# Scatters of routed rows, one at a time and spaced by TensorE's progress, in a metaformer layer with a mixture of experts

## The chip, the cores and the metric

One NeuronCore of a Trainium2 chip. The metric is the device time of one execution, in microseconds.

## The reference

```python
x = x + conv_ref(ln_c(x), ...)      # x is 2 x 256 x 96 x 96, float32
t = to_tokens(x)                    # 18432 tokens of 256 channels
t = t + ffn_ref(ln_t(t), ...)
# conv_ref: four branches, dilation 1, 4, 8, 12: a 3x3 convolution to 9 channels, softmax over
# the 9, then each pixel's 3x3 dilated patch weighted by them; [x, 4 branches] through a
# 1280 -> 256 projection, group norm (32 groups), relu
# ffn_ref: router to 8 experts, top 2 with weights normed to sum 1;
# expert: gelu(t @ w1[e] + b1[e]) @ w2[e] + b2[e]
```

## The kernel before

The program is written by hand, engine by engine, with semaphores between the engines. For each image m (0 and 1) there are two stages. The first norms the channels, makes the taps of the 36 filter channels, their softmax and the first fifth of the projection. The second, the convolution stage, has 64 steps (`STEPS`): each step weights the patches of one branch for one block of pixels on TensorE and projects the result. A step is made of units, four to six, 288 units (`UNITS`) per image; a unit ends with TensorE raising `out_ready`, after which ScalarE evicts it into `cat_hi` (L1423) and VectorE into `cat_lo` (L1941). Patches stand in a ring of 3 and are loaded by SyncE and, for part of them, by GpSimd (L2183, steps with `second_queue`), which waits until the unit `unit(s - RING + 1)` has left the ring's slot.

After the stages of both images comes the expert stage: a stream of 160 tiles (`STREAM`, 80 per image) of 256 routed rows. For a tile TensorE transposes the rows, multiplies by w1 and by w2; ScalarE does the gelu (L1468) and VectorE makes `h_lo` (L2016) and adds b2 into `e_out`, which has 4 slots; GpSimd scatters the 256 results in two indirect DMAs (`send`, L2205). A tile's time is counted as four units for the routing.

Beside these runs the routing of the tokens: image 0's during the second image's convolution stage (`plans[0]`, a slot each 3.25 units), image 1's during the first 80 tiles of the expert stage (`plans[1]`, a slot each 3.5 units). Six tiles of 128 tokens form a pair of groups (index p, 12 per image, 24 in all). A tile of tokens is transposed on TensorE, kept by ScalarE in `r_ln` (`keep_slot`, L1224), which has 3 slots (`HELD`) of one pair each, its two experts are chosen, and VectorE computes the destination rows (`r_pos`, L1703, then `r_placed`). `r_lnd` counts normed tiles. When a pair is placed, GpSimd writes each tile's rows twice (once per chosen expert) into `xs_dram` (named `expert_in`) by `scatter_rows`: 12 indirect DMAs per pair of 128 rows of 1040 bytes (L2127), 144 in each of the two stages. ScalarE's `keep_slot` of pair p + 3 waits until all twelve of pair p have landed (`r_scattered`). When an image's last pair is scattered, SyncE's `fill_ends` writes the ends of the experts' regions (L778) and `load_tile` (L791) loads the tiles. SyncE loads tile n in the program's order, once tile n - 3 has been used.

The order on GpSimd is set by `scatter_step` and `scatter_after`: a pair's scatters go out in thirds of four, each third in its own step of the convolution (behind that step's patch loads), or behind one tile's two output scatters.

Of the kernel before, what the change touches and what calls it, by code (L numbers as in the profile page):

```python
# [67 lines left out]
XROWS = IMAGES * XBLOCK  # L68
EARLY = 5
# [98 lines left out]
def build(nc, a):  # L168
    with ExitStack() as ctx:
# [418 lines left out]
        def loads(s):  # L588

            return (8, 5, 8, 18)[kind(s)]  # L590
# [1521 lines left out]
        def _(pool):  # L2112
# [7 lines left out]
            def scatter_rows(p, q):  # L2120

                if q == 0:
                    pool.wait_ge(r_placed, p + 1)
                    pool.wait_ge(r_lnd, TP * (p + 1))
                for k in range(4 * q, 4 * q + 4):
                    t, z = divmod(k, TOP)
                    pool.indirect_dma_start(out=xs_dram, out_offset=bass.IndirectOffsetOnAxis(ap=r_pos[:, p % HELD, z, t:t + 1], axis=0),  # L2127
                                            in_=r_ln[:, p % HELD, t], in_offset=None).then_inc(r_scattered[p % HELD], 16)

            for m in range(IMAGES):  # L2130
# [42 lines left out]
                def scatter_step(p, q):  # L2173

                    return step_of_tick[plans[0].placed(p)] + 3 + q

                thirds = 0
                for s in range(1, STEPS):
                    shared = [n for n in range(loads(s)) if second_queue(s, n)]
                    if shared and s >= RING:  # L2180
                        pool.wait_ge(out_ready, m * UNITS + unit(s - RING + 1))
                    for n in shared:
                        pool.dma_start(patch_target(s, n), patch_source(m, s, n)).then_inc(patch_pooled[s % RING], 16)  # L2183
                    while m and thirds < 3 * CPAIRS and scatter_step(thirds // 3, thirds % 3) <= s:
                        scatter_rows(thirds // 3, thirds % 3)
                        thirds += 1
# [3 lines left out]
            while thirds < 3 * CPAIRS:  # L2190
                scatter_rows(thirds // 3, thirds % 3)
                thirds += 1
# [7 lines left out]
            def send(n):  # L2200

                u, i = n % EO, n % ETILES
                pool.wait_ge(e_out_done, n + 1)
                for j in range(S // 128):
                    pool.indirect_dma_start(out=ys_dram, out_offset=bass.IndirectOffsetOnAxis(ap=e_dest[:, i, j:j + 1], axis=0),  # L2205
                                            in_=e_out[:, u, j], in_offset=None).then_inc(e_scattered[u], 16)

            def scatter_after(p, q):

                return plans[1].placed(p) // 4 - 1 + q  # L2210

            thirds = 0
# [46 lines left out]
```

## Time and profile before

| | us |
|---|---|
| median of 3 runs | 2258.05 |
| lowest, highest | 2256.24, 2268.76 |
| span of the profiled execution | 2561.4 |
| its convolution stage of image 1 | 628 |
| its expert stage with routing, tiles 13 to 77 | 497 |

The profile is of one execution of its own, recorded by the profiler, and its span runs from the first to the last instruction; for that execution no time other than the span is given. It is 303.3 us over the median, so every duration of the profile belongs to a longer execution than the runs whose median is shown. Engines are named as in the profile: PE is TensorE, PEld its weight load, DVE VectorE, ACT ScalarE, POOL GpSimd, SP SyncE. PEclk is the granted share of TensorE's full clock.

### The profile page before, as it was taken

What the parts mean: (1) busy time and instruction counts of PE and PEld (TensorE: products, weight loads), DVE (VectorE), ACT (ScalarE), POOL (GpSimd) and SP (SyncE); (2) the same over time, 40 slices, a digit from 0 to 9 for tenths busy, and PEclk for the clock granted to TensorE, in tenths of its full rate; (3) what the DMA queues carried; (4) which work ended last, traced back from release to release, by engine and by line L of the source; (5) the groups of instructions that cost most, each with busy time, mean ns of one, the idle gap of its engine ahead of it and who ended that gap; (6) DMA issues with size and microseconds to landing.
All of it is one profiled execution on the core that took longest, in us unless ns stands there. A gap on an engine that the chain in (4) does not pass through costs nothing.

```text
span 2561.4 us, 56574 instructions
## 1 busy us (share of the span) xinstructions
PE 2032.5 (79%) x20204; PEld 1920.6 (75%) x20204; DVE 1571.4 (61%) x4176; ACT 1336.8 (52%) x2869; POOL 1102.4 (43%) x1466
## 2 busy tenths in 40 slices
PE   5798899999699798878777776766676758988853
PEld 5788899999699787777777766666675657888842
DVE  5667665666577566546555554665665646766765
ACT  4576443333477545444444426665564637777732
POOL 4567122322276513433444442455655554444420
PEclk9899899999899888888787887887876869999975
DMA  5642455676443265556566567554554436777879
GB/s 172 220 127 76 140 157 144 166 174 172 119 142 111 81 192 176 161 163 170 183 181 182 157 213 237 164 171 154 174 174 152 152 121 228 252 257 255 276 267 369
DMA packets 340865, 459.86 MB, mean 180 GB/s; under 512 B 82749, under 2 KB 261437, under 8 KB 338237
## 3 DMA queue, kind: packets, MB, share of 16 engines
q1 hardware_dynamic: 229696, 245.14, 33.8%
q10 hardware_dynamic: 68433, 109.55, 12.8%
q0 software_dynamic: 42464, 101.56, 11.6%
q8 instruction: 168, 2.75, 0.5%
q14 instruction: 104, 0.85, 0.1%
HBM read 291.86 MB, written 174.69 MB: 182 GB/s over the span
## 4 chain that ended last, share of the span: by engine, by line
PE 47%; ACT 16%; another core or an unknown queue 9%; issue 8%; DVE 7%; DMA 6%; POOL 3%; ACTq 3%; SPq 1%; POOLq 1%; DVEq 0%
PE ps_y L426 15%; PE ps L426 7%; PE ps_a L426 6%; PE ps_o L1064 6%; PE ps_b L1001 4%; ACT e_act L1468 3%; ACT w_now L1479 3%; DMA o_acc<-res_scratch 2%; POOL taps L2147 2%; ACT h_hi L1471 1%; PE ps_tok L895 1%; PE ps_o L1051 1%; PE ps_k L846 1%; PE ps_a L939 1%
## 5 line engine op out<-in xcount | busy, mean ns | idle before, releaser
L426 PE MATMUL ps_y<-cat_hi,wp 128*128 128x288 f32 x2048 | 504.4, 322 | 10.9 <-issue 9.0
L2205 POOL DMA_INDIRECT expert_out<-e_out,e_dest x320 | 327.7, 1024 | 414.0 <-DVE e_out L2027 350.2
L2183 POOL DMA_DIRECT2D patches<-rows_scratch x348 | 194.7, 603 | 609.9 <-PE ps_o L1051 405.8
L426 PEld LDWEIGHTS ps_y<-cat_hi,wp 128*128 128x128 f32 x2048 | 370.6, 203 | 17.9 <-issue 15.9
L2127 POOL DMA_INDIRECT expert_in<-r_ln,r_pos x288 | 286.1, 993 | 114.0 <-issue 86.2
L2147 POOL TENSOR_TENSOR taps<-taps,g_rows 96x108 f32<-96x108 f32 (+3 forms) x440 | 259.9, 617 | 166.5 <-ACT g_rows L1303 162.6
L426 PE MATMUL ps<-w,h_hi 128*128 x1280 | 271.5, 309 | 75.7 <-DVE h_lo L2016 47.4
L1941 DVE SCALAR_TENSOR_TENSOR cat_lo<-ps_o,cat_hi 128x288 fp32r<-128x288 f32 (+1 forms) x576 | 228.0, 419 | 161.0 <-ACT cat_hi L1423 131.2
L426 PE MATMUL ps_y<-cat_lo,wp 128*128 128x288 f32 x1024 | 317.3, 310 | 6.3 <-issue 6.2
L1417 ACT ACTIVATE bands<-ps_b 112x288 f16<-112x288 f32 (+4 forms) x256 | 105.1, 411 | 406.3 <-PE ps_b L1001 325.9
L426 PE MATMUL ps<-e_hi,w_now 128*128 128x256 f32 x1280 | 283.9, 303 | 26.2 <-issue 21.3
L1423 ACT ACTIVATE cat_hi<-ps_o 128x288 fp32r<-128x288 f32 (+1 forms) x576 | 212.0, 384 | 169.5 <-remote 72.6
L426 PEld LDWEIGHTS ps<-w,h_hi 128*128 128x128 f32 x1280 | 214.1, 205 | 94.9 <-issue 94.6
L1933 DVE SCALAR_TENSOR_TENSOR bands<-ps_b,bands 112x288 f16<-112x288 f32 (+4 forms) x256 | 116.6, 455 | 245.8 <-ACT bands L1417 214.0
L1064 PE MATMUL ps_o<-bands,patches 112*128 112x72 f16 (+2 forms) x4608 | 214.2, 205 | 56.9 <-issue 32.0
L426 PEld LDWEIGHTS ps<-e_hi,w_now 128*128 128x128 f32 x1280 | 230.1, 208 | 35.0 <-issue 33.5
L2016 DVE TENSOR_TENSOR h_lo<-e_act,h_hi 128x512 fp32r<-128x512 f32 x160 | 110.4, 690 | 231.2 <-ACT h_hi L1471 190.2
L1468 ACT ACTIVATE e_act<-ps,b_of 128x256 f32<-128x256 f32 x320 | 133.8, 471 | 224.4 <-remote 149.6
L1064 PEld LDWEIGHTS ps_o<-bands,patches 112*128 112x128 f16 (+2 forms) x4608 | 186.9, 105 | 71.1 <-issue 67.9
L426 PEld LDWEIGHTS ps_y<-cat_lo,wp 128*128 128x128 f32 x1024 | 208.5, 204 | 4.3 <-issue 4.3
L1001 PE MATMUL ps_b<-filt_t,sel 94*128 94x32 f16 (+3 forms) x2592 | 172.7, 221 | 34.7 <-issue 26.4
L426 PE MATMUL ps<-w,h_lo 128*128 x640 | 189.0, 295 | 13.3 <-issue 13.1
(202 smaller groups left out, 4656.6 us busy)
## 6 DMA issues: line engine op xcount, KB each, us to landing
e_x<-expert_in SPq DMA_DIRECT2D x160, 260.0 KB
patches<-rows_scratch SPq DMA_DIRECT2D x160, 192.0 KB
patches<-rows_scratch SPq DMA_DIRECT2D x256, 108.0 KB
patches<-rows_scratch SPq DMA_DIRECT2D x192, 112.0 KB
x_in<-in_x SPq DMA_DIRECT2D x48, 384.0 KB, 3.6
rows_scratch<-rows_st SPq DMA_DIRECT2D x48, 384.0 KB, 4.3
r_x<-in_x ACTq DMA_DIRECT2D x72, 256.0 KB
r_y<-y_scratch ACTq DMA_DIRECT2D x72, 256.0 KB
```

Source lines behind the costliest of these rows:

```text
L426: mm = eng.matmul(out, lhs[p], rhs[q], start=start and n == 0, stop=stop and n == 2)
L1001: return pe.matmul(out, sel[:, b, 3 * y + x], pixels, start=True, stop=True, skip_group_check=True)
L1064: mm = pe.matmul(out, ring[:, (2 * p + z) * C + c * 128:(2 * p + z) * C + (c + 1) * 128], band_of[:, q, p * 72:(p + 1) * 72], start=k == 0 ...
L1423: act.activation(cat_pixels(cat_hi[:, s % 2, c], s, j), out_pixels(ps_o[:, n % 2], s), ACT.Copy, scale=UNSCALE).then_inc(cat_hi_done, 1)
L1468: last = act.activation(e_act[:, u, f], ps_1[:, u, f], ACT.Gelu, bias=b1_of[:, r, f, i:i + 1])
L1933: dve.scalar_tensor_tensor(out=bands[0:k, s % 2, 1, first:first + n], in0=ps_b[0:k, 0:n], scalar=0.0, in1=bands[0:k, s % 2, 0, first:first ...
L1941: dve.scalar_tensor_tensor(out=cat_pixels(cat_lo[:, s % 2, c], s, j), in0=out_pixels(ps_o[:, n % 2], s), scalar=UNSCALE, in1=cat_pixels(ca ...
L2016: dve.tensor_tensor(h_lo[:, u], e_act[:, u], h_hi[:, u].bitcast(F32), ALU.subtract).then_inc(h_lo_done, 1)
L2127: pool.indirect_dma_start(out=xs_dram, out_offset=bass.IndirectOffsetOnAxis(ap=r_pos[:, p % HELD, z, t:t + 1], axis=0), in_=r_ln[:, p % HE ...
L2147: last = pool.tensor_tensor(here, here, g_rows[:, u, first:end, i, b:b + nb].rearrange("p r b k -> p r (b k)"), ALU.add)
L2183: pool.dma_start(patch_target(s, n), patch_source(m, s, n)).then_inc(patch_pooled[s % RING], 16)
L2205: pool.indirect_dma_start(out=ys_dram, out_offset=bass.IndirectOffsetOnAxis(ap=e_dest[:, i, j:j + 1], axis=0), in_=e_out[:, u, j], in_offs ...
```

## The change

`scatter_rows`, which began four scatters in a row, becomes `scatter_row`, which begins one. In the convolution stage scatter k of pair p waits for `out_ready` to reach unit `placed(p) + 1 + 3k/2`, so two scatters of a pair stand 1 or 2 units apart; on GpSimd it is put before the first patch load that waits for a later unit. In the expert stage the scatters are put behind single output scatters: scatter k behind half tile 2 (placed/4 - 1) + 4k/5, so one or two behind each of nine half tiles; there they have no wait of their own but for the data. The wait for the normed rows is now one per tile of 128 rows. `ROWS_OUT` is `TP * TOP`, 12. Line numbers after 68 are higher by one or more.

```diff
-            def scatter_rows(p, q):
+            def scatter_row(p, k):

-                if q == 0:
+                t, z = divmod(k, TOP)
+                if k == 0:
                     pool.wait_ge(r_placed, p + 1)
-                    pool.wait_ge(r_lnd, TP * (p + 1))
-                for k in range(4 * q, 4 * q + 4):
-                    t, z = divmod(k, TOP)
-                    pool.indirect_dma_start(out=xs_dram, ...)
+                if z == 0:
+                    pool.wait_ge(r_lnd, TP * p + t + 1)
+                pool.indirect_dma_start(out=xs_dram, ...)
...
-                def scatter_step(p, q):
-                    return step_of_tick[plans[0].placed(p)] + 3 + q
-                thirds = 0
+                def scatter_unit(i):
+                    p, k = divmod(i, ROWS_OUT)
+                    return plans[0].placed(p) + 1 + 3 * k // 2
+                def paced_scatters(sent, before_unit):
+                    while sent < CPAIRS * ROWS_OUT and scatter_unit(sent) < before_unit:
+                        pool.wait_ge(out_ready, m * UNITS + min(scatter_unit(sent), UNITS))
+                        scatter_row(*divmod(sent, ROWS_OUT))
+                        sent += 1
+                    return sent
+                sent = 0
                 for s in range(1, STEPS):
                     shared = [n for n in range(loads(s)) if second_queue(s, n)]
+                    free_at = unit(s - RING + 1) if s >= RING else 0
+                    if m:
+                        sent = paced_scatters(sent, free_at)
                     if shared and s >= RING:
-                        pool.wait_ge(out_ready, m * UNITS + unit(s - RING + 1))
+                        pool.wait_ge(out_ready, m * UNITS + free_at)
                     for n in shared:
                         pool.dma_start(patch_target(s, n), patch_source(m, s, n)).then_inc(patch_pooled[s % RING], 16)
-                    while m and thirds < 3 * CPAIRS and scatter_step(thirds // 3, thirds % 3) <= s:
-                        scatter_rows(thirds // 3, thirds % 3)
-                        thirds += 1
...
-            def send(n):
+            def send(n, j):
                 u, i = n % EO, n % ETILES
-                pool.wait_ge(e_out_done, n + 1)
+                if j == 0:
+                    pool.wait_ge(e_out_done, n + 1)
+                pool.indirect_dma_start(out=ys_dram, ...)
+
+            def scatter_half(i):
+                p, k = divmod(i, ROWS_OUT)
+                return 2 * (plans[1].placed(p) // 4 - 1) + 4 * k // 5
+
+            sent = 0
+            for n in range(STREAM):
                 for j in range(S // 128):
-                    pool.indirect_dma_start(out=ys_dram, ...)
-            def scatter_after(p, q):
-                return plans[1].placed(p) // 4 - 1 + q
-            thirds = 0
-            for n in range(STREAM):
-                send(n)
-                while thirds < 3 * CPAIRS and scatter_after(thirds // 3, thirds % 3) <= n:
-                    scatter_rows(CPAIRS + thirds // 3, thirds % 3)
-                    thirds += 1
+                    send(n, j)
+                    while sent < CPAIRS * ROWS_OUT and scatter_half(sent) <= 2 * n + j:
+                        p, k = divmod(sent, ROWS_OUT)
+                        scatter_row(CPAIRS + p, k)
+                        sent += 1
```

The order on GpSimd in the convolution stage, before: a third's or two thirds' scatters in a row behind a step's patch loads (`x8` is eight in a row; `expert_in` is what the scatters write).

```order
L2127 DMA expert_in<-r_ln,r_pos 155648x260 x8
L2183 DMA patches<-rows_scratch 64x1x256 [waits out_ready]
L2183 DMA patches<-rows_scratch 64x1x256 x8
L2127 DMA expert_in<-r_ln,r_pos 155648x260 [waits r_lnd,r_placed]
L2127 DMA expert_in<-r_ln,r_pos 155648x260 x7
L2183 DMA patches<-rows_scratch 64x1x256 [waits out_ready]
L2183 DMA patches<-rows_scratch 64x1x256 x8
L2127 DMA expert_in<-r_ln,r_pos 155648x260 x4
```

The same place in the changed kernel:

```order
L2128 DMA expert_in<-r_ln,r_pos 155648x260 [waits r_lnd,r_placed,out_ready]
L2128 DMA expert_in<-r_ln,r_pos 155648x260 [waits out_ready]
L2128 DMA expert_in<-r_ln,r_pos 155648x260 [waits r_lnd,out_ready]
L2128 DMA expert_in<-r_ln,r_pos 155648x260 [waits out_ready]
L2128 DMA expert_in<-r_ln,r_pos 155648x260 [waits r_lnd,out_ready]
L2128 DMA expert_in<-r_ln,r_pos 155648x260 [waits out_ready]
L2128 DMA expert_in<-r_ln,r_pos 155648x260 [waits r_lnd,out_ready]
L2128 DMA expert_in<-r_ln,r_pos 155648x260 [waits out_ready]
L2196 DMA patches<-rows_scratch 64x1x256 [waits out_ready]
L2196 DMA patches<-rows_scratch 64x1x256 x8
L2128 DMA expert_in<-r_ln,r_pos 155648x260 [waits r_lnd,out_ready]
L2128 DMA expert_in<-r_ln,r_pos 155648x260 [waits out_ready]
```

Each scatter now has its own wait for `out_ready`, and a step's nine patch loads stand between two of them.

In the expert stage, before, for the first pair of image 1: four scatters behind each of three tiles' two output scatters (`expert_out`).

```order
L2205 DMA expert_out<-e_out,e_dest 45056x256 [waits e_out_done]
L2205 DMA expert_out<-e_out,e_dest 45056x256
L2127 DMA expert_in<-r_ln,r_pos 155648x260 [waits r_lnd,r_placed]
L2127 DMA expert_in<-r_ln,r_pos 155648x260 x3
L2205 DMA expert_out<-e_out,e_dest 45056x256 [waits e_out_done]
L2205 DMA expert_out<-e_out,e_dest 45056x256
L2127 DMA expert_in<-r_ln,r_pos 155648x260 x4
L2205 DMA expert_out<-e_out,e_dest 45056x256 [waits e_out_done]
L2205 DMA expert_out<-e_out,e_dest 45056x256
L2127 DMA expert_in<-r_ln,r_pos 155648x260 x4
```

The same pair in the changed kernel:

```order
L2214 DMA expert_out<-e_out,e_dest 45056x256 [waits e_out_done]
L2128 DMA expert_in<-r_ln,r_pos 155648x260 [waits r_lnd,r_placed]
L2128 DMA expert_in<-r_ln,r_pos 155648x260
L2214 DMA expert_out<-e_out,e_dest 45056x256
L2128 DMA expert_in<-r_ln,r_pos 155648x260 [waits r_lnd]
L2214 DMA expert_out<-e_out,e_dest 45056x256 [waits e_out_done]
L2128 DMA expert_in<-r_ln,r_pos 155648x260
L2214 DMA expert_out<-e_out,e_dest 45056x256
L2128 DMA expert_in<-r_ln,r_pos 155648x260 [waits r_lnd]
L2214 DMA expert_out<-e_out,e_dest 45056x256 [waits e_out_done]
L2128 DMA expert_in<-r_ln,r_pos 155648x260
L2128 DMA expert_in<-r_ln,r_pos 155648x260 [waits r_lnd]
```

One or two scatters stand behind each single output scatter, and the twelve reach over nine of these.

## Rows read from the trace of the kernel before

**Rows 1.** The page: its first line, and section 1, busy time of each engine.

```profile
span 2561.4 us, 56574 instructions
...
PE 2032.5 (79%) x20204; PEld 1920.6 (75%) x20204; DVE 1571.4 (61%) x4176; ACT 1336.8 (52%) x2869; POOL 1102.4 (43%) x1466
```

**Rows 2.** By stretch, its length; busy PE, PEld, DVE, ACT, POOL (count); PEclk, DMA share, GB/s.

```profile
274.00:647.00 373.00, 367.01 (x5649) 354.93 (x5646) 231.62 (x572) 148.95 (x412) 94.05 (x170) 1.00 0.63 162
...
895.00:1523.00 628.00, 509.51 (x6169) 474.08 (x6166) 355.53 (x1121) 272.78 (x735) 238.85 (x314) 0.83 0.61 174
...
1627.00:2124.00 497.00, 334.09 (x2252) 307.91 (x2252) 294.30 (x897) 273.12 (x503) 280.95 (x276) 0.77 0.50 160
...
2124.00:2454.00 330.00, 295.43 (x2415) 286.59 (x2416) 224.50 (x476) 248.98 (x430) 160.33 (x161) 0.97 0.76 249
```

**Rows 3.** The same view of line 1423 (`cat_hi`, one per unit), ScalarE.

```profile
274.00:647.00 373.00, 103.07 (x287) 1.00 0.63 162
895.00:1523.00 628.00, 107.59 (x285) 0.83 0.61 174
...
1007.00:1021.00 14.00, 3.67 (x9) 0.99 0.65 178
1106.00:1118.00 12.00, 2.85 (x8) 1.00 0.66 206
1144.00:1159.00 15.00, 3.62 (x11) 1.00 0.47 141
1274.00:1297.00 23.00, 4.91 (x13) 1.00 0.68 199
```

**Rows 4.** The same view of line 2016 (`h_lo`, one per tile), VectorE.

```profile
1582.00:1627.00 45.00, 6.12 (x10) 0.92 0.58 176
1627.00:2124.00 497.00, 44.64 (x65) 0.77 0.50 160
2150.00:2450.00 300.00, 51.15 (x74) 0.98 0.79 261
```

**Rows 5.** A burst: two stretches as in rows 2, and GpSimd's timeline.

```profile
1119.90:1134.40 14.50, 7.54 (x68) 5.56 (x67) 3.99 (x15) 1.29 (x4) 10.68 (x11) 0.74 0.60 174
1142.00:1144.00 2.00, 2.00 (x26) 1.85 (x26) 0.06 (x1) 0.50 (x2) 0.00 (x0) 0.53 0.44 143
...
1118.60 1.04 POOL L2127 DMA_INDIRECT expert_in<-r_ln,r_pos  x1 [0.30 <-issue]
...
1132.70 0.96 POOL L2127 DMA_INDIRECT expert_in<-r_ln,r_pos  x1 [0.30 <-issue]
```

**Rows 6.** Timeline of the same burst: start us, us, engine, line; in brackets the idle time before.

```profile
1124.32 0.27 PE L1064 MATMUL ps_o<-bands,patches 108*128 108x72 f16 x3 [0.53 <-issue]
...
1125.76 0.22 PE L1064 MATMUL ps_o<-bands,patches 108*128 108x72 f16 x2 [1.17 <-issue]
...
1128.68 0.49 ACT L1417 ACTIVATE bands<-ps_b 128x384 f16<-128x384 f32 x1 [7.05 <-remote]
...
1134.38 0.41 ACT L1423 ACTIVATE cat_hi<-ps_o 128x288 fp32r<-128x288 f32 x1 [5.21 <-remote]
```

**Rows 7.** Groups of instructions, 895 to 1523: busy us, mean ns, idle before it.

```profile
L2127 POOL DMA_INDIRECT expert_in<-r_ln,r_pos x144 | 142.6, 991 | 70.1 <-issue 42.4 <-DVE r_pos L1703 27.7
...
L2183 POOL DMA_DIRECT2D patches<-rows_scratch x170 | 96.2, 615 | 311.7 <-PE ps_o L1051 213.5 <-PE ps_o L1064 97.4 <-issue 0.8
```

**Rows 8.** Timeline at the end of the routing, GpSimd, then SyncE.

```profile
2101.40 0.97 POOL L2127 DMA_INDIRECT expert_in<-r_ln,r_pos  x1 [0.30 <-issue]
...
2110.11 10.02 SPq L778 DMA_DIRECT2D expert_in<-in_k_fill  x8
2123.99 2.56 SPq L791 DMA_DIRECT2D e_x<-expert_in  x3
```

**Rows 9.** Timeline: last scatter of a pair, and the reuse of its rows' slot.

```profile
1901.93 0.97 POOL L2127 DMA_INDIRECT expert_in<-r_ln,r_pos  x1 [0.30 <-issue]
...
1914.13 0.38 ACT L1224 ACTIVATE r_ln<-ps_k 128x256 f32<-128x256 f32 x1
```

More of the change, by code:

```diff
@@ L68 @@
 XROWS = IMAGES * XBLOCK
+ROWS_OUT = TP * TOP
 EARLY = 5
@@ L2119, in _ @@
             leave(pool)
-            def scatter_rows(p, q):
-                if q == 0:
+            def scatter_row(p, k):
+                t, z = divmod(k, TOP)
+                if k == 0:
                     pool.wait_ge(r_placed, p + 1)
-                    pool.wait_ge(r_lnd, TP * (p + 1))
-                for k in range(4 * q, 4 * q + 4):
-                    t, z = divmod(k, TOP)
-                    pool.indirect_dma_start(out=xs_dram, out_offset=bass.IndirectOffsetOnAxis(ap=r_pos[:, p % HELD, z, t:t + 1], axis=0),
-                                            in_=r_ln[:, p % HELD, t], in_offset=None).then_inc(r_scattered[p % HELD], 16)
+                if z == 0:
+                    pool.wait_ge(r_lnd, TP * p + t + 1)
+                pool.indirect_dma_start(out=xs_dram, out_offset=bass.IndirectOffsetOnAxis(ap=r_pos[:, p % HELD, z, t:t + 1], axis=0),
+                                        in_=r_ln[:, p % HELD, t], in_offset=None).then_inc(r_scattered[p % HELD], 16)
             for m in range(IMAGES):
@@ L2198, in _ @@
                     pool.dma_start(dst, src).then_inc(y_pooled, 16)
-            def send(n):
+            def send(n, j):
                 u, i = n % EO, n % ETILES
-                pool.wait_ge(e_out_done, n + 1)
-                for j in range(S // 128):
-                    pool.indirect_dma_start(out=ys_dram, out_offset=bass.IndirectOffsetOnAxis(ap=e_dest[:, i, j:j + 1], axis=0),
-                                            in_=e_out[:, u, j], in_offset=None).then_inc(e_scattered[u], 16)
-            def scatter_after(p, q):
-                return plans[1].placed(p) // 4 - 1 + q
-            thirds = 0
-            for n in range(STREAM):
-                send(n)
-                while thirds < 3 * CPAIRS and scatter_after(thirds // 3, thirds % 3) <= n:
-                    scatter_rows(CPAIRS + thirds // 3, thirds % 3)
-                    thirds += 1
+                if j == 0:
+                    pool.wait_ge(e_out_done, n + 1)
+                pool.indirect_dma_start(out=ys_dram, out_offset=bass.IndirectOffsetOnAxis(ap=e_dest[:, i, j:j + 1], axis=0),
+                                        in_=e_out[:, u, j], in_offset=None).then_inc(e_scattered[u], 16)
+            def scatter_half(i):
[3 more added lines that the diff above has]
+            for n in range(STREAM):
+                for j in range(S // 128):
+                    send(n, j)
[3 more added lines that the diff above has]
+                        sent += 1
             for u in range(HELD):
```

4 lines of the change are left out of this document (2 added, 2 removed).

## The prediction

> **What bounds the kernel now.** I read the page's sections 1 and 2 first, then the busy times by stage, then how many units of work each stage gets through. TensorE is busy 79% of a span of 2561.4 us, and no other engine is over 61%: TensorE is the bound wherever nothing else stops it [rows 1]. By stage it is not so even. The first image's second convolution keeps TensorE busy 367 of 373 us at the full clock (2.4 GHz). The second image's, the same products plus the routing's, takes 628 us with TensorE busy 510, at a mean granted clock of 0.83. The expert stage falls in two parts: 497 us with routing and scatters (TensorE busy 334, clock 0.77), then 330 us without routed-row scatters (busy 295 of 330, clock 0.97) [rows 2]. The reader is to see that both stretches that hold `scatter_rows` are those in which TensorE is neither busy nor at full clock.
>
> Counting makes it a rate. Each unit of the second convolution ends in one `cat_hi` eviction. Image 0 makes 287 of them in 373 us, 1.30 us each. Image 1 makes 285 in 628 us, 2.20 us each. In four stretches of image 1 without a scatter and at full clock it makes 9, 8, 11 and 13, 41 in 64 us, 1.56 us each, so the routing itself costs only 0.26 us a unit. The excess is 628 - 285 x 1.56 = **183 us** [rows 3]. In the expert stage one `h_lo` is one tile: 10 tiles in 45 us (4.5 us each) before the first scatter, 65 in 497 us (7.65 us each) with them. Excess 497 - 65 x 4.5 = **205 us** [rows 4]. Together 388 us lie on the 288 scatters.
>
> Where a burst runs, that excess can be seen. Twelve scatters start from 1118.60 to 1132.70, one each 1.27 us (0.97 busy and 0.30 between). In 14.5 us around them TensorE is busy 7.5 and ScalarE 1.3 [rows 5]. After about three scatters TensorE issues a few matmuls, then idles for "issue" (nothing that the profile shows) 0.5 to 1.2 us, again and again, and ScalarE stops for 7.0 and 5.2 us [rows 6]. The burst over, they go on at once; but TensorE's clock, which fell to half (1.2 GHz) during these idle pieces, is back at full only after 1142 [rows 5]. Pairs do no such thing: from 2150 to 2450 GpSimd begins two output scatters per tile, 4.05 us a tile (74 in 300 us), at clock 0.98 [rows 4].
>
> **How the profiled execution stands to the median.** The median is 2258.05, so this execution's span is 303.3 us longer than an ordinary run. The first image's convolution (busy 367 of 373) and the last 330 us (busy 295) have no room for it [rows 2]; of the stretches shown only those of the scatters have, with 388 us. If the other stretches last as long without the profiler, an ordinary run keeps at most 388 - 303 = **85 us** of the excess. What can it be? GpSimd's own work: a pair of tile groups takes 5.25 tiles in the expert stage (six slots of 3.5 units, four units a tile) and needs 12 + 10.5 scatters x 1.27 = 28.6 us of GpSimd, where TensorE needs 5.25 x 4.5 = 23.6 [rows 4, 5]. Over 12 pairs that is 60 us in which GpSimd would be the bound, profiler or not. The other 25 us may be burst stalls that ordinary runs have too.
>
> **The change, part by part.**
> - *Second convolution, image 1.* The 144 scatters stay, each now behind a wait for `out_ready`, at 1.5 units' distance: 2.3 us at 1.56 us a unit, against 1.27 in a burst. This is the spacing at which the output scatters of 2150 to 2450 (two per 4.05 us) leave TensorE alone. In the profiled execution I take off nine tenths of 183, 165 us, nearer to the pairs' row than to the burst's, since patch loads still stand beside the scatters; bounds are 0 (the stall belongs to each scatter, 144 x 1.3) and 183. In an ordinary run I take nine tenths of 25: **-22 us**; bounds 0 and, if all 85 are stalls that spacing cures, -85.
> - *The waits added there* cost nothing. Behind a waiting scatter stand only patch loads whose own wait is for a later unit (the order puts a scatter first only where its unit is below `free_at`), and GpSimd idles 311.7 us before them now [rows 7]. A patch load can start at most one scatter, 1.27 us, late; today up to twelve stand before it.
> - *The wait for all six `r_lnd`* becomes one per tile group of 128 rows. Placing is later than norming, so it gains nothing: 27.7 us of waits in this stage are for `r_pos` [rows 7], and GpSimd was early there.
> - *Expert stage.* Four scatters behind both output scatters of three tiles become one or two behind each output scatter of 4.5 tiles. That is 4.7 GpSimd operations a tile, 5.9 us of GpSimd against 4.5 of TensorE: still back to back, so still bursts by another name, cut only where `e_out` is awaited. GpSimd's 28.6 us per pair are the same. **0 us** in an ordinary run; bounds -60 (if its excess is stall and not GpSimd's time) and, below, a loss. In the profiled execution, half of the way from 497 to GpSimd's 65 x 28.6/5.25 = 354: -70.
> - *The end of routing.* The last pair's last scatter moves from tile 71's turn to tile 73's: 9 us later, or 3 x 1.27 = 3.8 us on a busy GpSimd. SyncE needs it before it loads tile 80, but first come its eight fills (10.0 us) and their landing (3.9), from 2110.11 to 2123.99, and the last scatter started at 2101.40 [rows 8]: 22.6 us of slack, 13 or more after the change. **0 us**, upper bound +9. At the first image's end the last scatter goes out at unit 277 of 288, where the last third went at unit 274; SyncE there waits for unit 278 and then fills too. 0 us.
>
> Sum for an ordinary run: 2258 - 22 + 0 + 0 = **2236 us**. For the profiled execution: 2561 - 165 - 70 = 2326, so the span should fall much more than the time.
>
> **A rule that speaks against the change.** In [rows 5] TensorE is busy 7.5 of 14.5 us beside the scatters, waiting for nothing that the profile names. The Trainium skill (SBUF — State Buffer, "two separate sides") says that engine ports and DMA ports are disjoint and that TensorE and ScalarE never wait on anyone there. By that rule the stalls are not made by the scatters' data or descriptors, and the spacing is worth 0: the sum would be 2258, the first rival below. By the rows alone it is worth up to 85. What the recording of a profile does to an engine is not in any row; the skill (NOTIFIC — the notification-queue block, 7.1 Overflow) says that its internal pipeline holds engines back rather than lose a record, which would put the whole stall on the profiler.
>
> **The rivals.**
> 1. *The stall exists only under the profiler.* For it: 303 of the 388 us must be absent from ordinary runs anyway, and the holes come without any wait. Against it: 85 us are left over, and 60 of them need GpSimd to be saturated, which in this trace it is not: 276 operations x 1.27 = 350 of 497 us [rows 2]. Time: 2258, no change, though the profile's span falls.
> 2. *The excess of the expert stage is a stall too, and spacing cures it.* For: the burst at a tile costs more than GpSimd's time, 7.65 against 5.4 us. Against: 4.7 scatters a tile remain nearly back to back. I take seven tenths of the 85, the rest for GpSimd's time. Time: 2258 - 85 x 0.7 = 2198.
> 3. *Slower: the row buffer comes free too late.* `r_ln` has three slots, and ScalarE's `keep_slot` of pair p+3 waits for pair p's twelve scatters. A pair's last scatter moves two tiles later, 2 x 4.5 = 9 us and up to three more output scatters in front, 3.8 us. Today the seventh expert pair's last scatter starts at 1901.93 and its slot is rewritten at 1914.13, 12.2 us later, 11.2 of which are left when it ends [rows 9]. 11.2 - 12.8 leaves -1.6, and landing comes on top (3.9 us from the last fill's issue to the load behind it [rows 8]): 1.6 + 3.9 = 5.5 us of wait for each of 9 pairs with a successor, 50 us if none of it is GpSimd's bound, with ScalarE holding `hidden` and so TensorE behind it. It decides as soon as the slack of a pair is under some 13 us. With the -22 the time is 2286, without them 2308. Against it: by the plan's ticks 9.5 units (2.4 tiles, 10.7 us) still lie between the output of the tile behind which the last scatter stands and the reuse, and where GpSimd is the bound ScalarE's wait costs nothing more.
>
> **How the numbers follow.** About 0.5% (11 us) is what a measurement here can tell from no change. Forecast (2236): 0.40. Rival 1 (2258): 0.33. Rival 2 (2198): 0.11. Rival 3 (2286 to 2308): 0.16. Faster by over 0.5%, under 2246.8: rival 2 and most of the forecast, 0.47. Within 0.5%: rival 1 and the forecast's weak end, 0.37. Slower: rival 3, 0.16. The range 2185 to 2287 holds the forecast with its bounds, rival 1, most of rival 2 and the low end of rival 3; it leaves out about 0.15.
>
> **What would show it.** Right: the scatters of the convolution start 2 us or more apart; the stage takes some 460 us instead of 628 with clock near 1.00; in the expert stage GpSimd has less idle time than the 147 us that 350 of 497 leave. Wrong: if the convolution stays over 550 us, a single scatter stalls TensorE and spacing is no cure. If the profile's span falls by 200 us and the time by less than 11, rival 1 holds. If ScalarE's idle time before `r_ln` L1224 grows and the expert stage is longer, rival 3 does. If the time falls by over 70 us, ordinary runs stall as the profiled one does, and my scaling from the 303 us was wrong.

## The result, and the profile after

| | before, us | changed, us | ratio, 95% interval |
|---|---|---|---|
| median, 4 runs each | 2258.24 | 2299.32 (2295.19 to 2302.53) | 1.017 [1.0144, 1.0197] |
| span of the profiled execution | 2561.4 | 2294.9 | |

The change costs 1.7%, 41 us. Yet the span of its profile is 266 us *shorter*. The two spans can't be compared. On three of the six chips of the experiments every run of the kernel before lay between 2534 and 2571 us, on the other three, as in the result, between 2251 and 2272. I call them the **burst-sensitive chips** and the **ordinary chips**; no chip was met twice, so whether the kind belongs to the chip or to the time of its use is not shown. The trace that the prediction reads (the expectations call it the trace read blind) is taken here as one of the first kind: its span is of that size, and it has the waits that mark that kind (below). Each ratio below is against the kernel before on the same chip. (The expectations of the first eleven experiments were written before this was known.)

First the profile after, on an ordinary chip: the page's first line and section 1.

```profile
span 2294.9 us, 56634 instructions
...
PE 1923.1 (84%) x20204; PEld 1842.0 (80%) x20204; DVE 1566.8 (68%) x4176; ACT 1333.1 (58%) x2869; POOL 1111.0 (48%) x1466
```

The busy times by stage of the same trace, columns as in [rows 2]: the second convolution, the expert tiles 12 to 79, the tiles 80 to 158.

```profile
898.00:1383.00 485.00, 442.15 (x6176) 422.32 (x6173) 354.18 (x1124) 271.93 (x738) 238.72 (x314) 0.95 0.80 223
1483.00:1897.00 414.00, 313.64 (x2358) 300.77 (x2358) 300.02 (x919) 280.12 (x519) 290.94 (x282) 0.88 0.61 197
1897.00:2190.00 293.00, 278.72 (x2341) 271.48 (x2341) 218.83 (x467) 242.16 (x419) 160.72 (x158) 0.99 0.82 275
```

And of the kernel before, unchanged, on an ordinary chip (the first experiment, span 2256.1):

```profile
898.00:1383.00 485.00, 442.47 (x6168) 422.86 (x6165) 353.28 (x1121) 271.48 (x737) 238.30 (x314) 0.95 0.79 223
1484.00:1858.00 374.00, 299.74 (x2362) 287.17 (x2361) 300.09 (x919) 281.53 (x519) 284.77 (x281) 0.92 0.68 217
1858.00:2151.00 293.00, 278.07 (x2345) 271.28 (x2344) 218.39 (x468) 243.36 (x420) 160.81 (x159) 0.99 0.83 276
```

This pair is the comparison. The convolution takes 485 us in both (628 in [rows 2]), the last tiles 293 in both. All of the loss lies in the expert stage with routing, 414 against 374 us: 40 us. What waits there is seen in the changed kernel's waits (engine, line, what it waited for: us in total, times, longest):

```profile
PEld ps_k L845 <- ACT r_ln L1225: 63.7, 27, 6.7
PE ps_k L845 <- ACT r_ln L1225: 56.9, 21, 6.5
...
ACT r_ln L1225 <- DMA expert_in<-r_ln,r_pos: 52.5, 9, 8.9
```

ScalarE waits nine times, 52.5 us, for a scatter to land before it may rewrite the slot of `r_ln`, and TensorE waits for ScalarE. The kernel before, on an ordinary chip, has three such waits:

```profile
ACT r_ln L1224 <- DMA expert_in<-r_ln,r_pos: 10.7, 3, 7.6
```

One such wait in the changed kernel's timeline, GpSimd, ScalarE, TensorE:

```profile
1685.16 0.97 POOL L2128 DMA_INDIRECT expert_in<-r_ln,r_pos  x1 [0.30 <-issue]
...
1688.70 0.38 ACT L1225 ACTIVATE r_ln<-ps_k 128x256 f32<-128x256 f32 x1 [8.91 <-DMA expert_in<-r_ln,r_pos]
...
1689.13 0.69 PE L845 MATMUL ps_k<-ident,r_x 128*128 128x128 f32 x2 [6.46 <-ACT r_ln L1225]
```

The pair's last scatter begins at 1685.16 and has landed by 1688.70; ScalarE had waited 8.9 us for it and TensorE then 6.5. Between the two lie 3.5 us; in [rows 9], for the pair after this one, it was 12.2.

Why does a wait of ScalarE cost time when GpSimd is the engine with the most to do? Because GpSimd then stands idle too. From the placing of the first expert pair to the ninth reuse of a slot, GpSimd's busy time, and what it waited for. The kernel before (269 us):

```profile
1486.00:1755.00 269.00, 219.80 (x1756) 211.01 (x1755) 224.76 (x711) 216.18 (x406) 204.06 (x201) 0.93 0.71 227
...
POOL expert_in L2127 <- issue: 32.9, 108, 0.3
POOL expert_out L2205 <- issue: 25.9, 85, 0.3
POOL expert_out L2205 <- DVE e_out L2027: 6.3, 8, 2.0
```

and the changed one (304 us):

```profile
1486.00:1790.00 304.00, 231.91 (x1751) 222.20 (x1750) 226.64 (x712) 214.10 (x402) 212.39 (x205) 0.88 0.63 205
...
POOL expert_out L2214 <- DVE e_out L2028: 35.6, 16, 5.0
POOL expert_in L2128 <- issue: 32.3, 106, 0.3
POOL expert_out L2214 <- issue: 24.7, 81, 0.3
```

Before, GpSimd is busy 204 us and spends 59 in the 0.3 us ahead of each scatter: 263 of 269 us. It is the bound of this stretch, and waits for `e_out` only 6 us. Changed, the same work stands beside 35.6 us of waits for `e_out`. The rows read as a circle: ScalarE waits for the pair's last scatter, TensorE for ScalarE, so no tile ends, and GpSimd has the next `e_out` to wait for.

### The profile page after: what moved, and what is told of

Same layout as the page of the kernel before. It is cut to its first block, busy times and chain, and to the rows that moved or that the text cites. A ratio compares the mean times of both kernels' runs of the same rounds, so it can differ in the third digit from the quotient of the medians.

```text
span 2294.9 us, 56634 instructions
## 1 busy us (share of the span) xinstructions
PE 1923.1 (84%) x20204; PEld 1842.0 (80%) x20204; DVE 1566.8 (68%) x4176; ACT 1333.1 (58%) x2869; POOL 1111.0 (48%) x1466
## 3 DMA queue, kind: packets, MB, share of 16 engines
q0 software_dynamic: 42464, 101.56, 13.0%
## 4 chain that ended last, share of the span: by engine, by line
PE 44%; DVE 13%; ACT 12%; DMA 10%; POOL 9%; issue 7%; ACTq 2%; SPq 1%; DVEq 1%; POOLq 1%
PE ps_y L427 16%; PE ps_a L427 7%; PE ps_o L1065 6%; PE ps_b L1002 4%; PE ps L427 4%; DMA out<-o_out 3%; POOL expert_in L2128 3%; POOL expert_out L2214 3%; ACT w_now L1480 3%; POOL taps L2148 3%; ACT e_act L1469 2%; DMA expert_in<-r_ln,r_pos 2%; PE ps_tok L896 1%; PE ps_a L940 1%; DMA e_x<-expert_in 1%
## 5 line engine op out<-in xcount | busy, mean ns | idle before, releaser
L427 PE MATMUL ps_y<-cat_hi,wp 128*128 128x288 f32 x2048 | 479.3, 310 | 1.8 <-DVE cat_lo L1942 1.8
L427 PEld LDWEIGHTS ps_y<-cat_hi,wp 128*128 128x128 f32 x2048 | 351.0, 193 | 2.0 <-DVE cat_lo L1942 2.0
L427 PE MATMUL ps_y<-cat_lo,wp 128*128 128x288 f32 x1024 | 306.2, 299 | 0.0
L427 PE MATMUL ps<-e_hi,w_now 128*128 128x256 f32 x1280 | 267.4, 293 | 4.9 <-ACT w_now L1480 2.6
L427 PEld LDWEIGHTS ps<-e_hi,w_now 128*128 128x128 f32 x1280 | 219.3, 200 | 6.2 <-issue 4.2
L1065 PE MATMUL ps_o<-bands,patches 112*128 112x72 f16 (+2 forms) x4608 | 196.2, 200 | 27.3 <-DVE cat_lo L1942 23.6
L1065 PEld LDWEIGHTS ps_o<-bands,patches 112*128 112x128 f16 (+2 forms) x4608 | 174.9, 102 | 34.1 <-issue 32.8
L427 PEld LDWEIGHTS ps_y<-cat_lo,wp 128*128 128x128 f32 x1024 | 198.0, 193 | 0.0
L427 PE MATMUL ps_a<-wg,xc_hi 128*96 128x324 f32 x768 | 180.8, 321 | 9.9 <-DVE xc_lo L1894 5.6
L427 PE MATMUL ps<-e_lo,w_now 128*128 128x256 f32 x640 | 185.2, 289 | 0.0
```

The lines of the kernel that those rows point to most:

```text
L427: mm = eng.matmul(out, lhs[p], rhs[q], start=start and n == 0, stop=stop and n == 2)
L1065: mm = pe.matmul(out, ring[:, (2 * p + z) * C + c * 128:(2 * p + z) * C + (c + 1) * 128], band_of[:, q, p * 72:(p + 1) * 72], start=k == 0 ...
```

## The experiments

**On ordinary chips: which part costs.**

The kernel before again, no edit.

> The kernel before once more, for a second trace. If its burst stalls belong to the recording of a profile, its median is 2258 within 10 us and the span of its profiled execution again some 300 us longer (2500 or more), while the changed kernel's span (2294.9) stood at its own median. If the 2561 us of the first trace were a single odd execution, this span is within 20 us of the median.

2259.68 us, 0.9985 [0.9969, 1.0001], span 2256.1: no 300 us come from recording. The stage rows are above.

The first half of the change alone (paced convolution, the expert stage's scatters in thirds):

```diff
-                for j in range(S // 128):
-                    send(n, j)
-                    while sent < CPAIRS * ROWS_OUT and scatter_half(sent) <= 2 * n + j:
-                        ...
+                send(n)
+                while thirds < 3 * CPAIRS and scatter_after(thirds // 3, thirds % 3) <= n:
+                    ...
```

> The changed pacing in the second convolution alone; in the expert stage the thirds of four as before. Theory A (the expert stage's last scatters come too late for the three slots of r_ln, 9 waits of 5.8 us): about 2245, since only that part was bad; at least 40 us below the changed kernel. Theory B (the waits on out_ready in the convolution cost TensorE time): 2299 or near it. Theory C (the single scatters between the two output scatters hold up e_out): like A.

2262.02 us, 0.9996 [0.9978, 1.0014]. The convolution part is worth nothing on an ordinary chip.

The other half alone (thirds by `scatter_step` in the convolution, single scatters by `scatter_half` in the expert stage):

> The single scatters of the expert stage alone, the convolution with its bursts as before. Theories A and C: some 50 us over the kernel before, 2310, with 9 waits of ScalarE before r_ln of 50 us in all. Theory B: 2258.

2301.06 us, 1.0158 [1.0133, 1.0182], and the same nine waits:

```profile
ACT r_ln L1224 <- DMA expert_in<-r_ln,r_pos: 50.7, 9, 9.0
```

The whole loss is the expert stage's. Is it that the last scatter is late, or that single scatters stand between the output scatters? Lateness without interleaving, thirds of four as before but two tiles later:

```diff
-            def scatter_half(i):
+            def scatter_after(p, q):
-                return 2 * (plans[1].placed(p) // 4 - 1) + 4 * k // 5
+                return plans[1].placed(p) // 4 - 1 + q + 2
```

> The paced convolution; in the expert stage thirds of four behind both output scatters as before, but each third two tiles later, so that a pair's last scatter stands where the changed kernel has it. Theory A (lateness alone): as slow as the changed kernel, 2290 to 2305, with the waits before r_ln there. Theory C (the interleaving is what costs): 2250.

2354.34 us, 1.0407 [1.0382, 1.0433]:

```profile
ACT r_ln L1225 <- DMA expert_in<-r_ln,r_pos: 98.9, 9, 15.6
```

Without interleaving the kernel loses 92 us, far above the expected 2290 to 2305, since the last scatter does not stand where the changed kernel has it but still later: for the first pair it begins at 1523.22 us, against 1516.02 in the changed kernel and 1509.56 before. Against the 10.7 us of waits that the kernel before has, the waits grow by 88 us here and by 42 in the changed kernel, and the times by 92 and 40. The reverse, interleaving without lateness:

```diff
-                return 2 * (plans[1].placed(p) // 4 - 1) + 4 * k // 5
+                return 2 * (plans[1].placed(p) // 4 - 1) + k // 2
```

> The changed kernel, its single scatters in the expert stage kept apart by half tiles, but spread over six half tiles (k // 2) in place of nine (4*k//5), so that the last of a pair starts about 1.5 tiles (5 to 6 us) earlier. Theory A (the r_ln slot is freed too late; 9 waits, 52.5 us, took the 40 us): the nine waits shrink to below 15 us together and the time is 2255 to 2268, no loss left. Theory C (scatters between the output scatters delay the outputs themselves or the queue, whatever their end): the loss stays, 2290 to 2302. In between, about 2275, would be both.

2261.04 us, 1.0005 [0.9992, 1.0017]:

```profile
ACT r_ln L1225 <- DMA expert_in<-r_ln,r_pos: 14.9, 5, 7.4
```

Moving the last scatter one and a half tiles forward gives back all 40 us. Now with nothing moved in time, only the wait cut in two (`TT` is 3, `TP` 6; a pair's scatters raise one semaphore for tiles 0 to 2 and another for 3 to 5):

```diff
-                    if k % TP == 0 and p >= HELD:
-                        act.wait_ge(r_scattered[p % HELD], 16 * TP * TOP * (p // HELD))
+                    if k % TT == 0 and p >= HELD:
+                        act.wait_ge(r_scattered[2 * (p % HELD) + k % TP // TT], 16 * TT * TOP * (p // HELD))
```

> The changed kernel with its pace untouched, but with two semaphores for each r_ln slot, one for the scatters of tiles 0 to 2 and one for tiles 3 to 5: the copy of a pair's first tile waits for the first six scatters of three pairs before alone, and its fourth tile for the last six. The last scatter of a pair is as late as in the changed kernel, but it is waited for three tiles later. Theory A: the waits of ScalarE before r_ln fall from 52.5 us to below 5 and the time is 2250 to 2265. Theory C (the cost is in the interleaving, not in the wait for the slot): 2290 to 2302 as before.

2267.52 us, 1.0039 [1.002, 1.0057]. The wait for the slot is nearly gone (4.1 us), and with it all but 9 us of the loss. These 9 us have no cause here: VectorE's wait for `e_out`, 9.7 us in the changed kernel, has grown to 29.6,

```profile
DVE e_out L2030 <- DMA expert_out<-e_out,e_dest: 29.6, 12, 5.1
...
ACT r_ln L1225 <- DMA expert_in<-r_ln,r_pos: 4.1, 2, 3.5
```

but it is as long (29.1 us) in the next experiment, which loses nothing.

> The kernel before with the same two semaphores for each slot. Its own trace still shows four waits of 0.5, 2.6, 0.6 and 7.6 us, 11 us together, before these copies. Theory A: they go, and the time is 2246 to 2256, 0.2 to 0.5% faster than before. If TensorE has its next work late for another reason (GpSimd, busy 49% of the span and more among the pairs), 2256 to 2264, nothing.

The same edit on the kernel before: 2259.73 us, 0.9997 [0.9981, 1.0013], and 1.000 [0.9978, 1.0023] on another ordinary chip (below). Its 11 us of waits go and it gains nothing, as fits a stretch in which GpSimd is busy throughout: a wait for the slot is free as long as GpSimd does not come to stand idle for it.

A burst of twelve in the convolution:

```diff
-                    return step_of_tick[plans[0].placed(p)] + 3 + q
+                    return step_of_tick[plans[0].placed(p)] + 4
```

> The kernel before, with all twelve scatters of a pair in a row in the second convolution (at the step where the second third was) in place of three thirds over three steps; the expert stage as before. If bursts of scatters hold TensorE up in a usual execution too (the reading of the odd trace: 4.4 us for an extra burst of four), twelve in a row cost at least 4 us a pair, 50 us for twelve pairs: 2290 to 2330. If the stall belonged to that one execution: 2255 to 2268, and the convolution of image 1 takes 484 to 488 us in its trace.

2260.85 us, 0.9997 [0.9981, 1.0014]. Its twelve scatters of the pair of [rows 5] run from 1106.40 to 1120.9. The busy times beside them, and of the whole stage:

```profile
1106.40:1120.90 14.50, 12.00 (x152) 11.24 (x151) 12.19 (x46) 7.34 (x20) 11.14 (x12) 0.96 0.90 235
898.00:1383.00 485.00, 440.63 (x6145) 421.51 (x6142) 355.11 (x1124) 268.80 (x730) 238.15 (x314) 0.96 0.81 225
```

In 14.5 us, beside twelve scatters here and eleven in [rows 5], TensorE is busy 12.0 us against 7.5, ScalarE 7.3 against 1.3. On an ordinary chip a burst of twelve costs no time that could be measured.

**On burst-sensitive chips.** Three experiments were run on one of them, beside a kernel before of 2563.08 us (11 runs, 2555.70 to 2571.16). Two put more work on GpSimd, the second with `p < CPAIRS`:

```diff
+                    for _ in range(2 if p >= CPAIRS else 0):
+                        if spins[0]:
+                            pool.wait_ge(spun, spins[0])
+                        pool.memset(spin[:], 0.0).then_inc(spun, 1)
```

> The kernel before, with two small memsets (128x48, each after a wait for the one before) behind each of the 144 routed scatters of the expert stage: more work for GpSimd alone, 288 instructions of some 0.1 to 0.3 us, so 30 to 90 us in all, about 12 x 2.5 to 7 us a pair. Theory A with GpSimd as the bound (in 1520 to 1750 us of the second trace of before GpSimd is busy for 176 of 230 us, and 0.3 us lies idle ahead of most of its 174 instructions, together nearly all): the time rises by about as much as GpSimd's work, one for one, 2285 to 2340, and the pairs take that much longer. Rival (GpSimd has room, only the place of the last scatter counts): less than half of the added work shows.

2539.77 us, 0.9915 [0.9888, 0.9942].

> The kernel before, with the same 288 memsets behind the 144 routed scatters of the second convolution. There TensorE is busy nearly all the time and GpSimd waits for its progress (292 and 155 us at the patch loads), so the added 30 to 90 us are hidden: 2255 to 2268. If GpSimd bound this stage too (the blind text's 28.6 us of GpSimd against 23.6 us of TensorE was for the expert stage alone), the time would rise as in the expert stage.

2515.48 us, 0.9802 [0.9772, 0.9832]. Neither theory had that: *more* work on GpSimd makes the program faster. In the second the twelve scatters of the pair of [rows 5] start over 16.9 us (1111.6 to 1128.5) instead of 14.1, and the convolution's last eviction comes at 1478 instead of 1523.

The third is the changed kernel with bursts of six in the expert stage (`k // 6` in place of `4 * k // 5`):

> The changed kernel, with a pair's twelve scatters of the expert stage in two bursts of six (k // 6) behind two following output scatters, in place of single ones over nine half tiles: denser than the thirds of before, the last one 3.5 tiles earlier than in the changed kernel. Theory A: no wait for the slot of more than a few us, 2252 to 2266, as before or a little under. If bursts hold TensorE up in the expert stage, or delay the outputs (the wait of VectorE for e_out, 29 us where the slot was no longer waited for): 2270 to 2300.

2469.69 us, 0.9634 [0.9609, 0.9659]. So the changed kernel itself had to be run on such a chip, with a new theory D: TensorE is held up there while GpSimd begins scatters in a row. It was run on a second one (before 2543.93, 7 runs).

> The changed kernel itself, again. Where the kernel before beside it takes 2250 to 2272 (as on the chips of the result and of the first eight experiments), the changed one takes 2290 to 2305. Where the kernel before takes 2550 to 2575 (as beside the last three experiments and in the trace read blind), theory D holds that TensorE is held up there while GpSimd begins scatters in rows: the second convolution falls from 628 to about 500 us, as in the trace with bursts of six (which has the paced convolution), and the expert stage falls too, so 2330 to 2440. Rival: the singles help there in the convolution alone, 2430 to 2480.

**2411.52 us, 0.9489 [0.9457, 0.952]: here the change gains 5.1%.** By stage:

```profile
898.00:1403.00 505.00, 452.51 (x6176) 429.88 (x6173) 354.67 (x1122) 271.58 (x738) 238.98 (x314) 0.94 0.76 215
1503.00:1993.00 490.00, 354.93 (x2369) 332.53 (x2368) 303.29 (x920) 283.72 (x522) 287.69 (x281) 0.80 0.53 167
1993.00:2304.00 311.00, 283.28 (x2348) 275.44 (x2347) 219.08 (x467) 243.94 (x420) 157.81 (x159) 0.98 0.78 259
```

The convolution is 505 us, 123 less than in [rows 2] and 20 above an ordinary chip. The expert tiles 12 to 79 still take 490, where the same kernel takes 414 on an ordinary chip. The last tiles, which have output scatters alone, take 311 against 293: the hold-up is not confined to the routed scatters. Its sign is in the waits, a releaser called "remote" on ScalarE (the page: "another core or an unknown queue") and "issue" on TensorE:

```profile
ACT e_act L1469 <- remote: 124.2, 28, 17.6
...
ACT r_ln L1225 <- remote: 48.4, 16, 9.5
...
PE ps L427 <- issue: 55.5, 74, 1.7
```

In the trace that the prediction reads they stand too:

```profile
ACT e_act L1468 <- remote: 149.6, 24, 18.9
...
PE ps L426 <- issue: 72.4, 99, 1.9
```

In the ordinary traces no wait is laid to "remote", and the last row reads

```profile
PE ps L426 <- issue: 3.7, 8, 0.9
```

in the kernel before. The transfers themselves are not slower: GpSimd's queue (q0) takes 11.6% of 2561 us of the 16 DMA engines' time in the one trace of the kernel before and 13.2% of 2256 us in the other, which is the same time for the same 42464 packets.

Nor did the pacing space the convolution's scatters evenly, as the 1 or 2 units between two of them suggest. GpSimd is still busy with a step's nine patch loads when the next scatters fall due, and then begins these in a row. In this trace:

```profile
1091.47 1.04 POOL L2128 DMA_INDIRECT expert_in<-r_ln,r_pos  x1 [0.30 <-issue]
...
1096.69 0.97 POOL L2128 DMA_INDIRECT expert_in<-r_ln,r_pos  x1 [0.30 <-issue]
1099.53 0.96 POOL L2128 DMA_INDIRECT expert_in<-r_ln,r_pos  x1 [1.87 <-PE ps_o L1065]
```

Five start from 1091.47 to 1096.69. Of the 132 distances between two scatters of a pair 65 are under 2 us here, and 79 on an ordinary chip. What the change did is to cut rows of up to twelve to rows of at most five here.

> The changed kernel with its single scatters in the expert stage over six half tiles (k // 2). Where before takes 2250 to 2272: 2255 to 2268, as before. Where before takes 2550 to 2575: by theory D the spacing is what counts and the wait for the slot costs nothing there (the last scatter ended 13 us or more ahead of the reuse), so within 30 us of the changed kernel, 2330 to 2450, and slower than it if closer scatters hold TensorE up more.

2431.96 us, 0.9555 [0.9514, 0.9595]: within the 30 us, and slower than the changed kernel, as D has it for closer scatters.

A third chip of this kind (before 2538.78, 7 runs) took the two halves apart.

> The paced convolution with the expert stage of before, again. Where before takes 2250 to 2272: no difference, ratio 0.998 to 1.002. Where before takes 2540 to 2575: the 123 us by which the convolution was shorter in the changed kernel's trace than in the trace read blind, so a ratio of 0.95 to 0.96, and the other 10 to 25 us of the changed kernel from the expert stage; a ratio above 0.975 would put most of the gain there.

**2424.52 us, 0.9539 [0.9501, 0.9578].** Nine tenths of the gain is the convolution's: 4.6% of the 5.1%. Its trace has the last eviction of the convolution at 1400 us, the changed kernel's at 1403, [rows 2]'s at 1523. With the paced convolution in all four, the expert tiles 12 to 79 take 536 us with a pair over two half tiles (the bursts of six), 513 over six (`k // 2`), 504 over six as thirds of four, and 490 over nine. By these, each a single trace and on three chips, the hold-up there goes with how densely a pair's scatters stand, and not with how many are begun between two output scatters.

> The changed kernel with two semaphores for each r_ln slot, again. Where before takes 2250 to 2272: ratio 1.004, as measured. Where before takes 2540 to 2575: the changed kernel had a ratio of 0.949 there with 9 us of waits for the slot and 48 us more that the trace lays to nothing on this core before the same copies; a ratio of 0.94 to 0.95 if only the 9 us go, below 0.94 if the 48 us belonged to this wait too.

2412.79 us, 0.9494 [0.9456, 0.9532]: the wait for the slot costs nothing there, and the 48 us of "remote" ahead of `r_ln` are not this wait (37.8 stay).

> The kernel before with two small memsets behind each routed scatter of the expert stage, again. Its trace on the other kind of chip gives their size: 1141 us of GpSimd in place of 1102, so 39 us busy, with the idle time around them perhaps 60. Where before takes 2250 to 2272: if GpSimd bounds the pairs there, the time rises by 30 to 70 us, 2290 to 2330; if it had room, by under 15, 2260 to 2275. Where before takes 2540 to 2575: ratio 0.99 as measured, since the memsets space the scatters.

2507.63 us, 0.9854 [0.9815, 0.9894]; once more faster for more work, and the ordinary chip's question still open. It was answered on a third ordinary chip (before 2259.33, 13 runs).

> The same kernel as in the two runs before it of this kind (two small memsets behind each routed scatter of the expert stage, 39 us of GpSimd in all). Where before takes 2250 to 2272: 2290 to 2330 if GpSimd bounds the pairs of the expert stage, 2260 to 2275 if it has room. Where before takes 2530 to 2575: a ratio of 0.985 to 0.992, as twice measured.

2288.17 us, 1.0112 [1.0064, 1.016]: 25 us by the ratio, 29 by the medians, just under the 2290 to 2330 expected of a bound and well over the 2260 to 2275 that room would leave. The memsets and the stretch of nine pairs, 288 us where it was 269:

```profile
L2136 POOL MEMSET spin<- 128x48 f32 x288 | 43.9, 152 | 8.3
...
1491.00:1779.00 288.00, 227.61 (x1751) 218.73 (x1749) 227.32 (x712) 214.61 (x403) 236.29 (x418) 0.90 0.66 214
```

GpSimd is busy 44 us more over the twelve pairs, 52 with the idle time ahead of the memsets, of which the shorter pauses ahead of the scatters give back some 20; the rest, 32 us, is nearly what the program pays. ScalarE's waits for the slot grow too (28.2 us, 8 times), but GpSimd waits only 2.0 us for `e_out` in that stretch, so they do not hold it back. That shows GpSimd as the bound of the pairs on an ordinary chip.

> The kernel before with two semaphores for each r_ln slot, again. Where before takes 2250 to 2272: ratio 0.998 to 1.002, as measured. Where before takes 2530 to 2575: no wait for the slot stands in the trace read blind, so no difference either, ratio 0.995 to 1.005.

2262.41 us, 1.000 [0.9978, 1.0023] (the split wait on the kernel before).

**No version beats both kernels on both kinds of chip.** Two come near: the paced convolution alone (0.9996 on an ordinary chip and 0.9539 on the other) and the changed kernel with six half tiles (1.0005 and 0.9555). On the second kind the full change has 0.9489; its interval overlaps theirs, but on its own chip it is 20 us faster than the six half tiles.

## Why the prediction was wrong

2236 us was forecast, 2185 to 2287, with 0.16 for slower; it is 2299. By its steps:

- **How the profiled execution stands to the median: failed, and the next terms hung on it.** The text found 303 us too many in that execution, took them for an effect of the profiler, and left an ordinary run "at most 85 us" of the hold-up. The first experiment has a span of 2256.1 under the same profiler. The 303 us are those of the other kind of chip. They are not all beside the routed scatters either: the stage that the text says has "no room" for them, the last tiles, gives 24 (318 us from tile 80 to the last `h_lo`, against 293). On an ordinary chip the hold-up is not 85 us but nothing in the convolution, whose 485 us are the same for thirds, single scatters and twelve in a row, and GpSimd's own work in the expert stage.
- **Convolution, -22: measured 0** (0.9996 and 0.9997). The bound "0" was the right end. Its other statement, that spacing cures a burst's stall where there is one, holds for the most part: nine tenths of 183, 165 us, were forecast for the profiled execution, and 123 came on a burst-sensitive chip. The distance of 2.3 us from scatter to scatter, on which the nine tenths rest, is there on average (2.5 us) but not one by one, as the text and the description of the change have it: half of the distances are under 2 us, up to five scatters stand in a row, and the stage takes 505 us where 460 were forecast. Evenly spaced scatters were not run.
- **Waits added in the convolution, 0: right.** Half the change alone shows no loss.
- **GpSimd as the bound of the pairs: right.** 28.6 us a pair were worked out; before, a pair takes 29.5 (269 us cover the placing and eight periods, 1518.5 to 1754.5), and added work is paid for.
- **Expert stage, 0: the failed term, measured +40.** The text gave it "below, a loss" with no size in the sum and the size in rival 3. For the profiled execution 70 us off 497 were forecast; between that trace and the changed kernel's on a burst-sensitive chip tiles 12 to 79 differ by 24 (514 and 490), of which 9 are there with the paced convolution alone.
- **End of routing, 0: right.** The last tiles take 293 us before and after.
- **Rival 3, slower, was what happened.** It said 9 waits of 5.5 us, 50 us, with ScalarE and TensorE held: measured 9 waits, 52.5 us, 5.8 each. Its time "without them 2308", with the convolution's -22 gone, is 9 us above the 2299 measured. It got 0.16 for two reasons that fell. "Where GpSimd is the bound ScalarE's wait costs nothing more" holds for the 11 us of the kernel before, and fails for the changed one, in which GpSimd then waits 35.6 us for `e_out`. And the 12.2 us of [rows 9] were read from a stretch in which TensorE was held up: TensorE late leaves the scatters slack. On an ordinary chip the same pair's last scatter begins at 1691.20 and the slot is rewritten at 1695.37, 4.2 us later, with no wait ahead of it, and some 3.5 to 6 us lie between the two where the changed kernel waits. So the wait was nearly due already, and any lateness had to show. That the 5.5 us a pair came out so near is in part luck. For the first pair the last scatter begins 6.5 us later than before (1509.56 and 1516.02), not 12.8, and stood 8.9 us ahead of the reuse (at 1518.45), not 12.2: both terms were too large, and they nearly cancel.
- **Rival 1 (2258)**: its time for the convolution is right, its cause wrong, since recording adds nothing to the span (2256.1 us beside a median of 2259.68). **Rival 2** (a stall in the expert stage cured by spacing) has nothing on an ordinary chip; on the other kind the whole change is 0.5% better than the convolution half, which the intervals don't part.
- **The rule on the two sides of SBUF** (the Trainium skill, SBUF — State Buffer, "two separate sides"), by which the spacing is worth 0, agrees with the ordinary chips (0.9996) and not with the outcome on the burst-sensitive ones, where spacing is worth 4.6%; whether the ports have a part in that no run here shows. The rule on a profiler's backpressure (the Trainium skill, NOTIFIC — the notification-queue block, 7.1 Overflow) has no case here: the spans of the profiled executions stand within 0.6% of the medians of their kernels on both kinds of chip.

What stays open: what differs in the burst-sensitive chips, and what "remote" stands for. The three were used one after another in time, between ordinary ones, so that something else than the chip differed then is not excluded. Shown is that more spacing shortens both stages there, and that the runs' times have it as well as the traces.

## What to carry to other kernels

Compare the span of a profile with the median before reading anything in it; if they differ by 13%, the profile is of another condition (here another kind of chip), and its slacks are not those of the timed runs: a stall elsewhere makes every buffer look free in time. Spread transfers only as far as the buffer they read from allows: beyond that the time grew by about as much as the waits for the buffer, and two thirds of the spreading (six half tiles in place of nine) cost nothing. Then look in the new trace whether the spacing is there: waits placed in an engine's program set the earliest start, and an engine that is behind begins its transfers in a row all the same. Where an engine is the bound, look at what makes it idle before calling a wait elsewhere free.

## What was not expected of the hardware

Of six chips that ran the kernel before in the experiments, three took 2251 to 2272 us and three 2534 to 2571, each kind with all its runs. On the second kind TensorE's granted clock over the run is 0.86 to 0.87 in place of 0.92, TensorE idles for "issue" 72 us ahead of one group of matmuls where an ordinary chip has 3.7, and waits appear whose releaser is "remote". It is strongest beside dense indirect DMAs begun by GpSimd. Small memsets behind these, which only add work, make the program 0.8 to 2% faster there; those of the expert stage make it 1.1% slower on an ordinary chip.
